# Stage 4 of a decoder kernel: score products that read 32 of the 128 rows

## The reference, cut to what matters

```python
def _L1_xattn_ref(x, mem, Wq, Wkv, Wout, bout):
    HEADS = 16
    h = HEADS; d = dim // h; scale = d ** (-0.5)         # d is 8
    q = x @ Wq
    xc = jnp.concatenate((mem, x), axis=1)               # 64 + 64 keys
    k, v = jnp.split(xc @ Wkv, 2, axis=-1)
    q, k, v = (to_heads(q), to_heads(k), to_heads(v))
    dots = jnp.einsum('bhid,bhjd->bhij', q, k) * scale
    mask = j_idx > i_idx + mem_len
    dots = jnp.where(mask[None, None], -jnp.inf, dots)
    attn = jax.nn.softmax(dots, axis=-1)
    out = jnp.einsum('bhij,bhjd->bhid', attn, v)
    return out.transpose(0, 2, 1, 3).reshape(b, n, dim) @ Wout + bout
```

## Time and profile before

| what | us |
|---|---|
| median of 3 runs | 904.66 |
| lowest and highest of them | 904.29, 908.63 |
| the profiled execution's own time | 906.1 |
| its span, first to last instruction | 904.3 |
| TensorE busy | 826.6 (91%) |
| VectorE, ScalarE, GpSimd busy | 538.3, 438.3, 91.7 |
| TensorE weight loads busy | 411.9 |
| mean granted TensorE clock | 0.977 of full speed |

### The profile page before, as it was taken

How to read it: one execution, slowest core, us unless ns; L and a number is a source line. 1 busy time by engine, 2 the same in 40 slices (tenths; PEclk the granted TensorE clock), 3 DMA queues, 4 the chain that set the end, 5 groups by cost and what they waited for, 6 DMA issues and landing times.

```text
span 904.3 us, 16120 instructions
## 1 busy us (share of the span) xinstructions
PE 826.6 (91%) x6069; PEld 411.9 (46%) x6069; DVE 538.3 (60%) x1205; ACT 438.3 (48%) x775; POOL 91.7 (10%) x74
## 2 busy tenths in 40 slices
PE   7999999997999779999967689999999989999997
PEld 4444444535555433343344454646555533443332
DVE  1634233335888766655578846676766667655653
ACT  3637373635677632343322426565646434554454
POOL 1360303021000000000024440000000000000000
PEclk9999999998999989999979999999999999999998
DMA  9300000000000000000000000000000000000000
GB/s 367 162 1 1 1 0 1 0 2 1 1 2 0 3 0 0 1 0 0 1 1 1 0 0 1 3 1 3 0 0 1 2 1 0 0 1 1 12 12 24
DMA packets 2363, 13.78 MB, mean 15 GB/s; under 512 B 257, under 2 KB 257, under 8 KB 1665
## 3 DMA queue, kind: packets, MB, share of 16 engines
q1 hardware_dynamic: 2304, 13.00, 3.6%
HBM read 11.95 MB, written 1.05 MB: 14 GB/s over the span
## 4 chain that ended last, share of the span: by engine, by line
PE 72%; DVE 13%; ACT 7%; issue 7%; DMA 1%; POOL 0%; DVEq 0%; ACTq 0%; SPq 0%
PE bank L2058 8%; PE bank L1679 5%; PE bank L2069 4%; PE bank L2221 4%; PE bank L1905 3%; PE bank L2147 3%; PE bank L1717 3%; PE bank L2200 3%; PE bank L2157 3%; PE bank L1730 3%; PE bank L1921 3%; PE bank L1910 3%; PE bank L2078 2%; PE bank L117 2%; PE bank L2136 2%
## 5 line engine op out<-in xcount | busy, mean ns | idle before, releaser
L2058 PE MATMUL bank<-sb_arena 128*64 128x256 f32 x512 | 82.4, 404 | 1.1 <-DVE sb_arena L1373 1.1
L1679 PE MATMUL bank<-sb_xT,sb_arena 128*128 128x512 f32 (+1 forms) x128 | 61.6, 613 | 3.5 <-ACT sb_arena L576 2.5
L829 ACT ACTIVATE sb_arena<-bank 128x512 f32<-128x512 f32 x64 | 37.7, 595 | 54.2 <-PE bank L2069 54.2
L1384 DVE TENSOR_REDUCE sb_rowmax<-bank 128x4 f32<-128x512 f32 x64 | 44.1, 690 | 30.7 <-PE bank L2058 30.0
L576 ACT ACTIVATE sb_arena<-bank 128x512 f32<-128x512 f32 x64 | 37.4, 597 | 36.2 <-PE bank L1679 36.1
L991 DVE TENSOR_TENSOR sb_arena<-bank,sb_arena 128x512 f32<-128x512 f32 x32 | 22.1, 690 | 50.2 <-PE bank L1730 49.9
L833 ACT ACTIVATE sb_arena<-sb_arena 128x512 f32<-128x512 f32 x64 | 40.3, 630 | 21.6 <-DVE sb_arena L1390 21.6
L728 ACT ACTIVATE sb_arena<-bank 128x512 f32<-128x512 f32 x36 | 21.4, 596 | 55.9 <-PE bank L1905 54.3
L1390 DVE TENSOR_TENSOR sb_arena<-bank,sb_rowmax 128x512 f32<-128x512 f32 x64 | 44.2, 691 | 2.5
L490 POOL TENSOR_TENSOR sb_arena<-sb_la,sb_consts 128x1024 f32<-128x1024 f32 x16 | 30.5, 1920 | 110.5 <-PE bank L1717 88.8
L2069 PE MATMUL bank<-sb_consts,sb_arena 128*128 128x128 f32 x256 | 40.9, 285 | 0.0
(11 more groups left out here) (333 smaller groups left out, 1681.7 us busy)
## 6 DMA issues: line engine op xcount, KB each, us to landing
sb_w<-w SPq DMA_DIRECT2D x1, 2646.5 KB, 27.0
sb_consts<-consts SPq DMA_DIRECT2D x1, 2236.0 KB, 14.3
sb_w<-w SPq DMA_DIRECT2D x1, 1736.0 KB, 20.2
sb_w<-w SPq DMA_DIRECT2D x1, 1175.0 KB, 8.3
sb_arena<-w SPq DMA_DIRECT2D x2, 512.0 KB, 4.2
sb_ctxT<-ctx SPq DMA_DIRECT2D x1, 1024.0 KB, 16.4
out<-sb_xT SPq DMA_DIRECT2D x4, 256.0 KB, 2.2
sb_xT<-x SPq DMA_DIRECT2D x1, 768.0 KB, 9.7
```

Source lines behind the costliest of these rows:

```text
L829: act.activation(probT4[k % 2][:, u % 4].rearrange("p j n -> p (j n)"), bank[2 + u % 2][:], ACT.Copy).then_inc(s_pt4, 1)
L1384: dve.tensor_reduce(rowmax4[u % 2][:], bank[(5, 0, 1)[u % 3]][:].rearrange("p (j t) -> p j t", j=4), AX, ALU.max).then_inc(s_mx4, 1)
L1679: pe.matmul(bank[h % 2][:], KT[:, h, :], cols(c), start=True, stop=True).then_inc(s_v, 1)
L2058: mm = pe.matmul(scored[64 * b:64 * b + 64, :, SEQ * half:SEQ * half + SEQ], qg4[:, g, q:q + SEQ], kx4[:, 2 * k + b, :, SEQ * half:SEQ * h ...
```

## The change

The two operands of a score product are cut to the 32 partitions of the head group g, on which alone `qg4[:, g]` is not zero. The row range of the array that the product uses goes from all 128 to the 32 that begin at 32g. The output's partitions, banks, columns, start and stop flags, the order of the instructions and all waits stay.

```diff
--- before.py
+++ after.py
@@ -2055,8 +2055,10 @@
                                   acausal128_bf[:, SEQ:].unsqueeze(1).to_broadcast([P, 4, SEQ]), start=True, stop=False)
                     for b in range(2):
                         q = (2 * k + b) * SEQ
-                        mm = pe.matmul(scored[64 * b:64 * b + 64, :, SEQ * half:SEQ * half + SEQ], qg4[:, g, q:q + SEQ],
-                                       kx4[:, 2 * k + b, :, SEQ * half:SEQ * half + SEQ], start=(half == 0), stop=True)
+                        mm = pe.matmul(scored[64 * b:64 * b + 64, :, SEQ * half:SEQ * half + SEQ],
+                                       qg4[32 * g:32 * g + 32, g, q:q + SEQ],
+                                       kx4[32 * g:32 * g + 32, 2 * k + b, :, SEQ * half:SEQ * half + SEQ],
+                                       start=(half == 0), stop=True)
                 mm.then_inc(s_s4, 1)
 
             def turn(u):
```

## The result

| | before | after |
|---|---|---|
| median of 6 runs each, us | 908.18 | 928.34 |
| lowest and highest | 904.29, 911.32 | 921.90, 949.10 |
| profiled execution, us | 906.1 | 923.69 |
| its span | 904.3 | 921.9 |
| mean granted clock | 0.977 | 0.955 |

The ratio of after to before is 1.0215 (95% interval 1.0166 to 1.0264): the kernel is 2% slower, some 20 us, where I had said no change. The ratios of this document leave out a run that is over 1.5% above the fastest of its kernel: here the one of 949.1, and the one of 917.2 of the experiment with half 0 on 32 rows. The 949.1 looks like more of the same effect: the mean clock of the whole program was 0.924 in it, against 0.943 to 0.956 in the other five.

The account below looks back on a forecast made before the run. TensorE was taken to bound stage 4, with nothing covering a loss. All terms were 0 except -0.7 us from shared rounds; from the median 904.66 this gave 904.0 us, range 897 to 907.

Parts of the forecast that it names:

- What bounds the kernel: Stage 4: TensorE, busy 178.1 of 181.6 us, never pauses; VectorE waits for the scores, and nothing covers a loss.
- Step 1: Score products: each row still streams 256 moving columns against 64 stationary ones, and fewer partitions stream no faster; change 0.
- the rival of the clock: Stage 4: clock falls to half because products leave most of the array unused; up to +90 us, chance 0.04.
- Step 2: Switches between score products and full-array instructions: still four per unit at about 0.10 us; no difference, ends -26 and +26 us.
- Step 5: Neighbouring units' head groups on different rows share a round at five places, 0.21 us each; -0.7 us, from 0 to -1.05.
- the signs of being wrong: Stage 4: a half under 0.55 or at 1.0 us, mask 0.1 later, or the stretch's clock under 0.95.
- Step 3: Second weight load of each half, late after a change of shape: unchanged; at best it vanishes, -6.8 us.
- Step 4: Products of b = 0 and b = 1 keep their different column halves and still run together; change 0.
- The pairs: Each half of score products: two 32-row products cannot run together, four rounds instead of two; +55 us, chance 0.05.

Follow-up runs that it names:

- the pairs: Against the kernel before: two units at a time, both whole-bank masks first, then eight 32-row products with two head groups adjacent; 880.41 us, ratio 0.9698.

## Why the prediction was wrong

- **What bounds the kernel**: right. TensorE sets the pace of stage 4 and nothing covers a loss. What the low clock cost in the stage went into the total: 15.8 of the 17.6 us of span.
- **Step 1, columns, "Change: 0"**: right for each instruction at a given clock and wrong as the whole account of what fewer rows do. This is the step that failed, together with the rival of the clock, to which I gave 0.04. I had priced it at up to +90 us and put it aside because "the rows say that standstill brings it down, and there is none". Rows 9 show a fall right behind a standstill. They don't show that nothing else brings one, and I read them so. In the changed kernel the clock fell at 609.4 with TensorE busy for 3.40 of 3.40 us in both stretches ahead. Measured: 41 us of the stage at half clock in the profiled execution. The gains of steps 2 and 5 below come to 2.8 us at most, so that it cost up to 15.8 + 2.8 = 18.6 us, 0.45 us for each us at half clock. The range ended at 907 and left the case out. Of the signs of being wrong that I had named, only this one came: the clock of the stretch under 0.95.
- **Step 2, changes of shape**: right, nearly. A product of 32 rows and 64 columns switches like one that is narrow in one direction only. It leaves the array a trifle sooner: the half goes from 0.585 to 0.58, about 0.6 us over 128 halves.
- **Step 3, the late weight load**: right, the 0.05 stays: the second pair of rows still starts 0.27 us behind the first. That it is the weight load that is late stays an inference. It fits that rows with 128 stationary columns are longer by twice as much behind a change of shape (1.12 us for two rows in place of 1.02).
- **Step 4, side by side**: right. The pairs didn't fall apart; at 601.49 four products even ran together.
- **Step 5, different row groups**: right in mechanism, half the size. I counted one shared round at a place (0.21 us). The eight rows lost two (0.43): 5 places are 2.1 us, less what VectorE keeps in the first chunk.
- **The rivals**: the clock was the true one, and its price of +90 was a bound for a fall that lasts the whole stage. It lasted a fifth of it.
- **The base**: I counted from 904.66, the median of three runs. Six runs gave 908.18, 3.5 more, so that a change worth nothing would have fallen outside the range of 897 to 907 as well. The loss of 20 us doesn't come from that.

What settles the cause is the order of kernels that differ in the rows that the score products address and in the full-array mask work between them:

| kernel | rows, half 0 and half 1 | clock of the score stretch | us at half clock in it | clock of the whole program: mean, lowest and highest (executions) |
|---|---|---|---|---|
| before | 128, 128 | 1.00 | 0 | 0.975, 0.971 to 0.981 (33) |
| half 0 on 32 | 32, 128 | 1.00 | 0 | 0.974, 0.964 to 0.980 (4) |
| half 1 on 64 | 32, 64 | 0.94 | 20.5 | 0.967, 0.961 to 0.970 (4) |
| changed | 32, 32 | 0.89 | 41.0 | 0.946, 0.924 to 0.956 (6) |
| changed, mask twice | 32, 32 | 0.94 | 23.9 | 0.964, 0.961 to 0.966 (4) |
| changed, mask first over the bank | 32, 32 | 0.96 | 13.6 | 0.968, 0.964 to 0.973 (10) |

Third and fourth column are of one profiled execution each; the fourth adds up twice the missing share of the clock over pieces of 1.7 us. The last column holds periods of low clock of the other stages too, but it is of every execution, and it gives the same order. How far the clock falls also changes from run to run: without the one of 949.1 the changed kernel's runs spread over 13 us, those before over 7.

Three things stay open. Whether the stationary or the moving operand's rows count, since in these kernels both come from the same partitions. Whether it is the rows or the shape, since no experiment had few rows and all columns (half 1 on 64 rows with the same 64 columns, 0.94 for 0.89, speaks for the rows). And what the gap at the stage's start adds: in all five kernels whose clock falls, the first fall begins about 2 to 5 us behind that start, and in four of them it holds over half of the low time (23.8 of the changed kernel's 41 us, all of it with the mask first and in the pairs). The gap isn't needed for every fall, as the four later ones of the changed kernel show, and not enough for one, as the kernel before shows; it may help.

## What to carry to other kernels

Cutting a product to the partitions that hold data gained nothing by itself here: at the same clock a half of 32-row products took the time of one of 128-row products (0.58 us), and in this stage, which TensorE bounds, it cost 2% through the clock. It paid here where products of different row groups were made neighbours, with the full-array work gathered ahead of them. The same 32-row operands then took 3.0% off the time (0.9698), 1% more than that order with 128 rows. Before that, look at changes of the array's shape: putting the mask first saved 0.9% with no narrow product at all.

## What the runs showed of the hardware that I had not expected

- In stage 4 of this kernel the granted clock falls to half on a TensorE that is busy without a pause, when score products of 32 rows take the place of those of 128 (0.89 over 190 us). Zeros in the data don't do it (1.00). The Trainium skill ("TensorE: Matmul & The Clock Gate", "Why this matters for your kernels") ties a drop in throughput to idle gaps between bursts of matmuls. The fall of the earlier trace rows agrees with it; the fall at 609.4 us, with TensorE busy for 3.40 of 3.40 us ahead of it, shows that keeping gaps away wasn't enough.
- Float32 products in two row groups and two column halves run four at a time: eight MATMUL rows in 0.59 us in place of 1.02, sixteen in 1.03 in place of 1.88. The Trainium skill ("TensorE: Matmul & The Clock Gate", Part 3) says that products in distinct row groups run concurrently, and these rows agree.
